# Attention's entry: q and k read from PSUM by DVE in pairs of tiles, parts turned by strips

## What is computed

```
q = (x @ wq).reshape(B, T, 16, 16)          # x is the normalized input
k = (x @ wk).reshape(B, T, 4, 16)
v = (x @ wv).reshape(B, T, 4, 16)
...
q = q * cos + _rotate_half(q) * sin
k = k * cos + _rotate_half(k) * sin
scale = 1.0 / jnp.sqrt(16)
scores = einsum('bhqd,bhkd->bhqk', q, k) * scale
p_g = softmax(where(causal, scores, neg)); p_l = softmax(where(local, scores, neg))
out = 0.5 * (p_g @ v + p_l @ v)
```

## Time and profile before

| | |
|---|---|
| median of 3 runs | 1564.37 us (1563.4 to 1566.02) |
| the profiled execution | 1572.69 us, its span 1570.9 us |
| mean granted TensorE clock | 0.923 of 2.4 GHz |
| busy share of the span | PE 85%, DVE 72%, ACT 58%, POOL 28% |

### The profile page before, as it was taken

How to read it: one execution, slowest core, us unless ns; L and a number is a source line. 1 busy time by engine, 2 the same in 40 slices (tenths; PEclk the granted TensorE clock), 3 DMA queues, 4 the chain that set the end, 5 groups by cost and what they waited for, 6 DMA issues and landing times.

```text
span 1570.9 us, 39585 instructions
## 1 busy us (share of the span) xinstructions
PE 1332.1 (85%) x15736; PEld 797.0 (51%) x15816; DVE 1128.3 (72%) x1823; ACT 907.6 (58%) x1527; POOL 435.1 (28%) x415
## 2 busy tenths in 40 slices
PE   5688888899789999998846889888987999999985
PEld 3533322345466666666625333323454666666663
DVE  4678981545599999996566677633376999999937
ACT  3524447544578777884326245563355888888741
POOL 4799930132122222222124000002312222222201
PEclk9678999899899999999967799998997999999998
DMA  5000001300722222221010000000016222222100
GB/s 167 1 2 3 1 2 36 107 1 14 135 50 61 53 53 53 53 59 38 1 54 2 29 2 2 2 1 27 1 52 111 57 54 53 57 60 57 42 1 27
DMA packets 37614, 62.04 MB, mean 39 GB/s; under 512 B 15088, under 2 KB 25072, under 8 KB 36992
## 3 DMA queue, kind: packets, MB, share of 16 engines
q1 hardware_dynamic: 37216, 58.44, 15.8%
q10 hardware_dynamic: 288, 2.10, 0.3%
HBM read 19.75 MB, written 7.01 MB: 17 GB/s over the span
## 4 chain that ended last, share of the span: by engine, by line
PE 52%; DVE 16%; issue 13%; ACT 12%; POOL 2%; DVEq 2%; DMA 1%; POOLq 1%; ACTq 0%; SPq 0%
DVE region L1195 5%; PE PS L1585 4%; PE PS L1695 4%; PE PS L1647 4%; PE PS L1707 4%; PE PS L1834 3%; PE PS L1819 3%; PE PS L1850 3%; ACT L1024 3%; PE PS L1597 3%; PE PS L1867 2%; PE PS L1943 2%; PE PS L1627 2%; DVE S L1390 2%; PE PS L1873 2%
## 5 line engine op out<-in xcount | busy, mean ns | idle before, releaser
L791 POOL TENSOR_TENSOR region<-region 128x1024 f32<-128x1024 f32 x64 | 155.2, 2426 | 517.1 <-DVE region L1378 517.1
L886 ACT ACTIVATE region<-PS 128x512 f32<-128x512 f32 x288 | 164.7, 597 | 130.7 <-PE PS L1647 88.8
L1195 DVE TENSOR_REDUCE region<-PS 128x1 f32<-128x512 f32 (+3 forms) x304 | 180.7, 652 | 69.1 <-PE PS L1600 44.2
L1834 PEld LDWEIGHTS PS<-region 64*64 64x64 f32 x4096 | 136.8, 135 | 40.0 <-issue 40.0
L1834 PE MATMUL PS<-region 64*64 64x64 f32 x4096 | 154.4, 224 | 0.0
L1597 PE MATMUL PS<-region 96*128 96x512 bf16 (+3 forms) x384 | 117.7, 358 | 25.2 <-DVE region L1195 17.3
L1647 PE MATMUL PS<-region 99*128 99x512 bf16 x288 | 112.6, 412 | 19.8 <-ACT region L886 19.0
L1383 DVE TENSOR_TENSOR region<-region 128x1024 f32<-128x1024 f32 x64 | 117.6, 1838 | 0.0
L1375 DVE SCALAR_TENSOR_TENSOR region<-region,rows 128x1024 f32<-128x1024 f32 x64 | 82.2, 1284 | 45.1 <-DMA region<-region 26.7
L1002 ACT ACT_TABLE_LOAD x60 | 77.0, 1283 | 61.9 <-PE PS L1794 35.6
L728 POOL TENSOR_TENSOR coef<-var,power 128x4 f32<-128x4 f32 (+2 forms) x16 | 16.2, 1011 | 340.1 <-DVEq L1112 340.1
(11 more groups left out here) (258 smaller groups left out, 2935.6 us busy)
## 6 DMA issues: line engine op xcount, KB each, us to landing
region<-region SPq DMA_DIRECT2D x256, 128.0 KB, 2.4
region<-parts_scratch SPq DMA_DIRECT2D x8, 448.0 KB, 9.8
X<-in_L_attn_x_dram SPq DMA_DIRECT2D x2, 1024.0 KB, 5.7
region<-in_L_ffn_factors_dram SPq DMA_DIRECT2D x2, 1024.0 KB, 7.0
out_dram<-X SPq DMA_DIRECT2D x4, 512.0 KB, 2.9
parts_scratch<-region SPq DMA_DIRECT2D x2, 768.0 KB, 4.3
w_in_s<-in_L_attn_W_in_dram SPq DMA_DIRECT2D x1, 1216.0 KB, 7.9
region<-in_L_ffn_W_fc_dram SPq DMA_DIRECT2D x1, 1024.0 KB, 6.1
```

The lines of the kernel that those rows point to most:

```text
L791: nc.gpsimd.tensor_tensor(PB1[:, r], PB1[:, r], PB2, ALU.add).then_inc(s_bb, 1)
L886: nc.scalar.activation(PB[:, u % (2 * G0), :], PS[:, 2 + u % 2, :], ACT.Exp).then_inc(s_p, 1)
L1195: nc.vector.reduce_max(MB[:, h:h + nh, k0 // 4], src, AX).then_inc(s_smu, 1)
L1834: last = mm(PS[q, 2 + half, (i % 4) * P + 64 * c:(i % 4) * P + 64 * c + 64], PB1[q, r, t], PC1[q, r, t], start=True, stop=True, tile_posit ...
```

## The change

The tiles are taken two at a time. DVE reads q and k of both tiles from PSUM (banks 4 and 5), without ACT's copies to SBUF. The scale 1/4 is split: the tables for cos and sin, for q and k alike, are multiplied by 1/2 on the host. The parts stand in one tile `SP` with four slots per head: first part, first part again, second, third. DVE writes slots 0, 2 and 3; ACT copies slot 0 into slot 1. PE then turns, per head, three pieces of two adjacent slots (32 columns each) into the three 32-row strips of the 96 rows, with a tile position per strip: 60 turns of 32 columns per tile instead of 20 of 96. `Q_PARTS` and `K_PARTS` say which slots make the strips; their six products are the same six as before, in another order. POOL has no part in the entry any more. ACT copies v of both tiles in two instructions, after DVE has read q and k (`s_rd`), and q's two banks in one. PE projects the next pair only when v of the pair before has been copied (`s_vv`), and turns the pair before it behind that.

```
-QX_BANKS = ((0, 1, 2), (3, 6, 7))
+QX_BANKS = ((0, 2), (6, 3))
+Q_PARTS = (1, 0, 2)
+K_PARTS = (1, 2, 0)
...
-        QK = sb("QK", [P, 2, 20, D0])
-        RA = sb("RA", [P, 20, D0])
-        RB = sb("RB", [P, 20, D0])
-        SP1 = sb("SP1", [P, 2, 20, D0], BF16)
...
-        QX = sb("QX", [P, 2, 20, 6, D0], BF16)
+        RA = sb("RA", [P, 2, 20, D0])
+        RB = sb("RB", [P, 2, 20, D0])
+        SP = sb("SP", [P, 2, 2, 20, 4, D0], BF16)
+        arena.used = spare_at + 4160
...
                 root(b, "att", rstd)
-                for i in range(NT):
-                    r = i % 2
-                    pool.wait_ge(s_spl, b * NT + i + 1)
...
-                        last = nc.gpsimd.tensor_copy(dst, src)
...
-                        nc.gpsimd.tensor_copy(dst, part[:, r, 0:H0, :].unsqueeze(2))
-                    pool.drain().then_inc(s_qx, 1)
-
...
-                        nc.scalar.mul(QK[:, i % 2, 0:H0, :], bank[:, 0:256].rearrange("p (h d) -> p h d", d=D0), float(D0) ** -0.5)
...
-                        nc.scalar.copy(dst, SP1[:, n % 2, 0:H0, :].unsqueeze(2).to_broadcast(list(dst.shape))).then_inc(s_qxq, 1)
...
+                def copy_v(t):
+
+                    act.wait_ge(s_rd, b * NT // 2 + t + 1)
+                    for dst, c in ((V, 320), (VW, 384)):
+                        last = nc.scalar.copy(dst[:, 2 * t:2 * t + 2, :, 0:D0],
+                                              PS[:, 4:6, c:c + 64].rearrange("p t (h d) -> p t h d", d=D0))
+                    last.then_inc(s_vv, 1)
+
+                def copy_parts(n):
+
+                    q, k = QX_BANKS[n % 2]
+                    act.wait_ge(s_qxt, b * NT + n + 1)
+                    nc.scalar.copy(QT[0:SPLIT, :, n * P:(n + 1) * P],
+                                   PS[0:SPLIT, q:q + 2, :].bitcast(BF16).rearrange("p b (h t) -> p (b h) t", h=8))
+                    nc.scalar.copy(KT[0:SPLIT, :, n * P:(n + 1) * P],
+                                   psb(k)[0:SPLIT, 0:4 * P].rearrange("p (h t) -> p h t", h=4)).then_inc(s_qt, 1)
+
+                for t in range(NT // 2):
+                    copy_v(t)
+                    act.wait_ge(s_sp, b * NT // 2 + t + 1)
+                    nc.scalar.copy(SP[:, t % 2, :, :, 1], SP[:, t % 2, :, :, 0]).then_inc(s_dup, 1)
+                    if t > 0:
+                        copy_parts(2 * t - 2)
+                        copy_parts(2 * t - 1)
+                copy_parts(NT - 2)
+                copy_parts(NT - 1)
...
+                for t in range(NT // 2):
+                    r, half = t % 2, D0 // 2
+                    dve.wait_ge(s_qkv, b * NT + 2 * t + 2)
+                    qk = PS[:, 4:6, 0:320].rearrange("p t (h d) -> p t h d", d=D0)
+                    bc = lambda a, x, e: a[:, 2 * t:2 * t + 2, x:e].unsqueeze(2).to_broadcast([P, 2, 20, e - x])
                     nc.vector.tensor_tensor(RA[:], qk, bc(cosq, 0, D0), ALU.mult)
...
+                    nc.vector.tensor_tensor(RB[:, :, :, half:], qk[:, :, :, 0:half], bc(sinq, half, D0),
+                                            ALU.mult).then_inc(s_rd, 1)
                     dve.drain()
                     nc.vector.tensor_tensor(RA[:], RA[:], RB[:], ALU.add)
                     dve.drain()
-                    nc.vector.tensor_copy(SP1[:, r], RA[:])
+
+                    dve.wait_ge(s_qxt, b * NT + max(2 * t - 2, 0))
+                    nc.vector.tensor_copy(SP[:, r, :, :, 0], RA[:]).then_inc(s_sp, 1)
                     dve.drain()
...
+                    nc.vector.tensor_tensor(SP[:, r, :, :, 3], RB[:], SP[:, r, :, :, 2], ALU.subtract)
                     dve.drain().then_inc(s_spl, 1)
...
+                def turn_parts(n):
+
+                    q, k = QX_BANKS[n % 2]
+                    pe.wait_ge(s_spl, b * NT // 2 + n // 2 + 1)
+                    pe.wait_ge(s_dup, b * NT // 2 + n // 2 + 1)
+                    pe.wait_ge(s_qt, b * NT + max(n - 1, 0))
+                    for h in range(20):
+                        to = psb(q + h // 8 if h < H0 else k)[:, (h % 8) * P:(h % 8 + 1) * P]
+                        for g, part in enumerate(Q_PARTS if h < H0 else K_PARTS):
+                            src = SP[:, n // 2 % 2, n % 2, h, part:part + 2, :].rearrange("p s d -> p (s d)")
+                            last = tr(to[32 * g:32 * g + 32, :], src, identb[:], tile_position=(0, 32 * g))
+                    last.then_inc(s_qxt, 1)
+
+                for t in range(NT // 2):
+                    if t > 0:
+                        pe.wait_ge(s_vv, b * NT // 2 + t)
+                    for i in (2 * t, 2 * t + 1):
+                        project_qkv(i)
+                    if t > 0:
+                        for n in (2 * t - 2, 2 * t - 1):
+                            turn_parts(n)
+                for n in (NT - 2, NT - 1):
+                    turn_parts(n)
+
+                pe.wait_ge(s_w, 16 * NLOAD)
                 pe.wait_ge(s_qt, (b + 1) * NT)
...
-        ident=np.eye(P, dtype=np.float32), cos=by_tile(cos), sin=by_tile(sin), masks=masks,
+        ident=np.eye(P, dtype=np.float32), cos=by_tile(np.float32(0.5) * cos), sin=by_tile(np.float32(0.5) * sin), masks=masks,
```

More of the change, by code:

```diff
@@ L353, in build @@
         s_qkv = sem("qkv_ready")
-        s_qk = sem("qk_copied")
+        s_rd = sem("qk_read")
+        s_sp = sem("first_parts_ready")
+        s_dup = sem("first_parts_doubled")
         s_vv = sem("v_copied")
         s_spl = sem("split_ready")
-        s_qx = sem("kx_ready")
-        s_qxq = sem("qx_ready")
         s_qxt = sem("qx_transposed")
@@ L744, in _ @@
                 root(b, "att", rstd)
-                for i in range(NT):
-                    r = i % 2
-                    pool.wait_ge(s_spl, b * NT + i + 1)
-                    pool.wait_ge(s_qxt, b * NT + max(i - 1, 0))
-                    nc.gpsimd.tensor_tensor(touch[:], onesc[:], onesc[:], ALU.mult)
-                    kx = QX[:, r, H0:20]
-                    for dst, part in (
-                        (kx[:, :, 0:1, :], SP1), (kx[:, :, 3:4, :], SP1), (kx[:, :, 5:6, :], SP1),
-                        (kx[:, :, 1:2, :], SP2), (kx[:, :, 4:5, :], SP2), (kx[:, :, 2:3, :], SP3),
-                    ):
-                        src = part[:, r, H0:20, :].unsqueeze(2)
-                        last = nc.gpsimd.tensor_copy(dst, src)
-                    qx = QX[:, r, 0:H0]
-                    for dst, part in ((qx[:, :, 3:4, :], SP2), (qx[:, :, 4:5, :], SP2), (qx[:, :, 5:6, :], SP3)):
-                        nc.gpsimd.tensor_copy(dst, part[:, r, 0:H0, :].unsqueeze(2))
-                    pool.drain().then_inc(s_qx, 1)
                 if b == 0:
@@ L1163, in _ @@
                 dve.wait_ge(s_first, 16 * NFIRST)
[L1165 to L1173 removed]
+                for t in range(NT // 2):
[3 more added lines that the diff above has]
+                    bc = lambda a, x, e: a[:, 2 * t:2 * t + 2, x:e].unsqueeze(2).to_broadcast([P, 2, 20, e - x])
                     nc.vector.tensor_tensor(RA[:], qk, bc(cosq, 0, D0), ALU.mult)
[L1175 to L1176 removed]
+                    nc.vector.tensor_tensor(RB[:, :, :, 0:half], qk[:, :, :, half:], bc(sinq, 0, half), ALU.mult)
+                    nc.vector.tensor_tensor(RB[:, :, :, half:], qk[:, :, :, 0:half], bc(sinq, half, D0),
+                                            ALU.mult).then_inc(s_rd, 1)
                     dve.drain()
@@ L1543, in _ @@
                 transposed(b, 0)
-                for i in range(NT + 2):
-                    if i < NT:
-                        bank = PS[:, 4 + i % 2, :]
-                        pe.wait_ge(s_qk, b * NT + max(i - 1, 0))
-                        for k in range(KC):
-                            mm(bank[:, 0:384], XT[:, k, i * P:(i + 1) * P], wqkv[:, k, :], start=k == 0, stop=k == KC - 1)
-                        if i == 0:
-                            for row, n, t0 in ((0, 32, 0), (32, 32, 16), (64, 64, 48)):
-                                for k in range(KC):
-                                    last = mm(bank[row:row + n, 384:448], XT[:, k, t0:t0 + n], wqkv[:, k, 320:384],
-                                              start=k == 0, stop=k == KC - 1)
-                        else:
-                            for k in range(KC):
-                                last = mm(bank[:, 384:448], XT[:, k, i * P - 16:i * P + 112], wqkv[:, k, 320:384],
-                                          start=k == 0, stop=k == KC - 1)
-                        last.then_inc(s_qkv, 1)
-                    if i >= 2:
-                        n = i - 2
-                        pe.wait_ge(s_w, 16 * NLOAD)
-                        pe.wait_ge(s_qx, b * NT + n + 1)
-                        pe.wait_ge(s_qxq, b * NT + n + 1)
-                        pe.wait_ge(s_qt, b * NT + max(n - 1, 0))
-                        for h in range(20):
-                            last = nc.tensor.transpose(psb(QX_BANKS[n % 2][h // 8])[0:SPLIT, (h % 8) * P:(h % 8 + 1) * P], QX[:, n % 2, h].rearrange("p s d -> p (s d)"), identb[:])
```

(15 more changed lines are left out.)

43 lines of the change are left out of this document (2 added, 41 removed).

## The result

| | before | changed |
|---|---|---|
| median | 1565.19 us (1563.4 to 1566.37, 4 runs) | 1549.81 us (1549.0 to 1550.17, 4 runs) |
| ratio | | 0.9902, 95% interval 0.9885 to 0.9919 |
| profiled execution, its span | 1572.69, 1570.9 | 1549.0, 1547.2 |
| first entry, second entry | 47.09, 46.26 | 39.52, 38.09 |
| mean granted clock | 0.923 | 0.929 |

The account below looks back on a forecast made before the run. The prediction took ACT's 4.16 us per tile to bound the old entry loop. Gains of 8.54 and 7.92 less 1.6 made 14.9: 1557.8 on the profiled execution, 1549.5 us for the median, 8.3 below; range 1544 to 1560.

Parts of the forecast that it names:

- The sum: Both entries: 8.54 us gained in the first batch, 7.92 in the second, less 1.6 for one clock fall: 14.9.
- ACT's 4.16: Old entry loop: ACT's step from one tile's first copy to the next, 4.16 us, taken as what sets the pace.
- the chain's POOL: Old entry loop: the chain of waits runs through POOL's last copies for a tile; removing those alone would gain little mid-loop.
- The price of strips: PE's turns in the entry: the three strips overlap, so a tile's 60 turns take 1.3 us.
- The other end, 3.4: PE's turns in the entry: strips taken one after another, 3.4 us a tile; as a rival 1565.0 us, chance 0.06.
- DVE from PSUM at no charge: DVE's reading of q and k in the entry: PSUM costs nothing extra, 0.82 us for 640 elements.
- Rival (D): Entry: prices on DVE and ACT too low, full-rate casts 1.05 us and q copies 2.6 per batch; 1551 to 1557, chance 0.12.
- The added wait: Entry: a projection waits until DVE has read and ACT has copied V of the pair before; named as late next.
- The schedule: First batch's entry, timed pair by pair: first product for the row maxima at 56.52 instead of 65.06 us.
- The clock: Entry: PE has only turns for 4 us between pairs 2 and 3; one fall in two batches, 1.6 us deducted.
- Rival (A): Entry: the clock stays at 1.2 GHz throughout, ending slower than before at 1571.2 us; chance 0.09.
- Rival (C): First attention: 61 us of slack at the ternary weights hides the first batch's gain; 1556.5 us, chance 0.01.

Follow-up runs that it names:

- its second run: The changed kernel itself, unedited, run again as the base for the follow-up edits: 1549.75 us, 0.9891 of the kernel before.
- both other places of the doubling: Changed kernel with the copy of slot 0 into slot 1 done by DVE (1543.31 us), or by ACT behind the pair's first turned tile's copies (1544.38 us).

## Why the prediction was right

- **The sum.** From the end of tile 1's projection the forecast was 8.54 + 7.92 - 1.6 = 14.9 us less, and 14.4 was measured. That the median came within 0.3 us of the forecast is partly luck: the interval of the ratio is 5 us wide, and the median of before in the later jobs lies between 1563.45 and 1567.69.
- **What bounds the old loop.** ACT's 4.16, against the chain's POOL: shown, by the step that stayed 4.16 without POOL's copies.
- **The price of strips.** 1.3 a tile, taken from the earlier trace rows: shown (1.30 for 60, 2.41 for 120). The other end, 3.4, measured 2.92.
- **DVE from PSUM at no charge**, and the strided casts at half the full rate: shown, 824 and 481 ns, 494 for the cast. Rival (D) has nothing left; the q copy took 1.86 where 1.85 was forecast.
- **The added wait and ACT's queue.** The schedule placed V of pair 2 and tile 3's turn behind two tiles' copies, and pair 3 15.58 behind the end of tile 1's projection; 15.75 was measured. The order of work was read rightly, so the sum held. What taking the tiles in pairs is worth by itself was not tried.
- **The words beside it were wrong**: "ACT without gaps from the second pair on". ACT waits 1.05, 0.84 and 1.05 ahead of its doublings in the first entry, and V of one pair follows V of the pair before by 6.58 and 6.87 us, not 6. Each wait was in the schedule as a time (first part 32.93, doubled by 33.72), but was not seen as something that could be had back. It was worth 2.3 us an entry.
- **A slip in the signs**: the second entry was to end near 845, but that leaves out the gain of the first; with it the schedule gives 845.34 - 8.54 = 836.8. It ended at 830.17; most of the rest is the 6.9 us between the entries.
- **The clock.** Right in size: one fall in the two batches, deducted at 1.6; pair 1 took 5.30 instead of 3.62, so 1.7. Wrong in place: it was to fall between pairs 2 and 3, where every run showed 1.00, and fell at pair 1 of the first entry. There it doesn't always fall: it did in the changed kernel, its second run and the run with the doubling on POOL, and not in four others that added no products, whose work ahead of it is nearly the same (turns strip by strip, ACT's copies of q and k, both other places of the doubling). What decides it is open. That tile 7 is turned at 1.2 GHz held: 4.57 for 120 turns instead of 2.41, with PE idle 3.95 ahead of them.
- **Rival (A)** fell with it: pairs 2 and 3 were projected at 1.00 in both batches. The rule from TensorE: Matmul & The Clock Gate in the Trainium skill, section Part 4: PE-mode transpose, that transposes don't lift the clock, would have the clock fall where turns alone run. The turns strip by strip don't bear it out: turns alone for 12 us, with 0.52 idle, kept 1.00. In the changed kernel the turns that ran at 0.50 came behind 3.52 and 3.95 us of idle PE.
- **Rival (C)** fell: POOL's work behind the ternary weights came 11.15 us earlier, more than the 8.06 of the entry, so nothing was hidden there.

## What to carry to other kernels

A chain of waits names the last releaser: look in each engine's own timeline for the step from tile to tile, and price that. An engine that waits in every pair can still be the bound, by its order: look for an instruction that waits for a late producer with finished work queued behind it, and change places before moving work to another engine. Measure an edit from a point behind everything that it doesn't touch: here 1.3 us of the gain, and the whole of a seeming 1.9, lay in a projection ahead of the edits. When PE works by strips of 32 columns, let the innermost loop run over the strips.

## What the runs showed of the hardware

- 120 turns of 32 columns took 2.41 us with neighbours on different strips and 5.84 with neighbours on the same one, at a granted clock of 1.00 both times.
- Through two stretches of turns alone, 5.84 and 5.82 us with 0.52 idle between, the granted clock stayed at 1.00.
- f32 products on DVE took as long from PSUM as from SBUF: 824 and 826 ns for 640 elements, 481 and 485 for 320.
- A bf16 copy of 640 elements on POOL made DVE's subtraction beside it 0.54 us longer (0.83 to 1.37); the same copy on DVE costs 0.32, less than the 0.72 on POOL or the 0.73 on ACT.
- Behind the second entry of the changed kernel the clock was granted at 0.50 up to 852 us, although PE was busy 7.53 and 9.29 of 10 us in the last two windows. Products that held it at 1.00 through the first entry only moved the fall: it was 0.50 again from 64 to 76, with PE busy 11.08 of 12.
